# Seven half products for the down projections of combinations 8 to 30, with the rows of two token blocks kept in DRAM

## The reference

```python
x = x + attention(layernorm(x), Wq, bq, Wk, bk, Wv, bv, Wbeta, bbeta, Walpha, balpha)
xt = layernorm(x).reshape(2048, 512)
Wg, Wu, Wd = (LUT[codes] * scales for gate, up, down)      # 4096x512, 4096x512, 512x4096
gate, up = xt @ Wg.T, xt @ Wu.T                            # 2048 x 4096 each
inter = gelu_tanh(gate) * up
x = x + inter @ Wd.T
```

## Time and profile before

| | |
|---|---|
| median of 3 runs | 1143.35 us (1142.88 to 1143.51) |
| span of the profiled execution | 1141.7 us |
| TensorE busy | 1134.5 us, 99% |
| VectorE busy | 709.7 us, 62% |
| GpSimd busy | 553.2 us, 48% |
| ScalarE busy | 450.9 us, 39% |
| chain of work that ended last | 96% TensorE |

### The profile page before, as it was taken

How to read it: one execution, slowest core, us unless ns; L and a number is a source line. 1 busy time by engine, 2 the same in 40 slices (tenths; PEclk the granted TensorE clock), 3 DMA queues, 4 the chain that set the end, 5 groups by cost and what they waited for, 6 DMA issues and landing times.

```text
span 1141.7 us, 20153 instructions
## 1 busy us (share of the span) xinstructions
PE 1134.5 (99%) x8086; PEld 795.0 (70%) x8086; DVE 709.7 (62%) x1306; ACT 450.9 (39%) x1045; POOL 553.2 (48%) x542
## 2 busy tenths in 40 slices
PE   9999999999999999999999999999999999999999
PEld 5666655565467777777777777777777777777786
DVE  7788656367777855665566556655665566555564
ACT  4433334253344434343434343434343434343432
POOL 3386535155783945363636353625362536255430
DMA  8021111000101010101010101010101010000012
GB/s 305 2 76 45 31 38 38 10 10 1 56 19 38 20 38 20 38 19 38 20 37 20 38 19 38 20 37 19 38 21 33 19 36 27 30 18 19 29 38 75
DMA packets 22830, 41.99 MB, mean 37 GB/s; under 512 B 2704, under 2 KB 3024, under 8 KB 22736
## 3 DMA queue, kind: packets, MB, share of 16 engines
q1 hardware_dynamic: 22736, 40.70, 10.9%
HBM read 36.46 MB, written 4.23 MB: 36 GB/s over the span
## 4 chain that ended last, share of the span: by engine, by line
PE 96%; DVE 2%; POOL 1%; issue 0%; DMA 0%; ACT 0%; SPq 0%; DVEq 0%; ACTq 0%; POOLq 0%
PE ps L560 45%; PE ps L665 27%; PE ps L390 8%; PE ps L521 7%; PE ps L625 2%; PE ps L356 1%; PE ps L482 1%; PE ps L465 1%; PE ps L489 1%; PE ps L476 1%; PE ps L400 1%; PE ps L456 1%; DMA WR<-wqkv 0%; POOL bigA L1479 0%; DVE wf L1285 0%
## 5 line engine op out<-in xcount | busy, mean ns | idle before, releaser
L560 PE MATMUL ps<-REG,WR 128*128 128x256 f16 x1344 | 183.3, 273 | 0.0
L560 PE MATMUL ps<-XT,WR 128*128 128x256 f16 x1344 | 183.3, 273 | 0.0
L1302 DVE TENSOR_TENSOR load<-load,ps 128x256 f32<-128x256 f32 x168 | 70.6, 420 | 171.0 <-PE ps L560 100.6
L665 PE MATMUL ps<-WR,ihl_s 128*128 128x512 f16 x720 | 173.0, 379 | 0.0
L665 PE MATMUL ps<-WR,vv 128*128 128x512 f16 x660 | 159.7, 379 | 0.0
L942 ACT COPY load<-ps 128x256 f32<-128x256 f32 x168 | 62.6, 372 | 245.8 <-PE ps L560 245.8
L560 PEld LDWEIGHTS ps<-REG,WR 128*128 128x128 f16 x1344 | 131.4, 98 | 37.5
L560 PEld LDWEIGHTS ps<-XT,WR 128*128 128x128 f16 x1344 | 131.5, 98 | 15.4
L1302 DVE TENSOR_TENSOR bigB<-bigB,ps 128x256 f32<-128x256 f32 x168 | 70.5, 420 | 114.9 <-ACT bigB L942 87.2
L942 ACT COPY bigB<-ps 128x256 f32<-128x256 f32 x168 | 62.6, 373 | 168.8 <-PE ps L560 168.8
L665 PEld LDWEIGHTS ps<-WR,ihl_s 128*128 128x128 f16 x720 | 70.4, 98 | 62.6
(11 more groups left out here) (202 smaller groups left out, 1890.4 us busy)
## 6 DMA issues: line engine op xcount, KB each, us to landing
load<-codes SPq DMA_DIRECT2D x48, 256.0 KB
load<-scales SPq DMA_DIRECT2D x48, 256.0 KB
y<-X SPq DMA_DIRECT2D x15, 256.0 KB, 2.1
bigA<-cla SPq DMA_DIRECT2D x14, 256.0 KB, 3.1
X<-x SPq DMA_DIRECT2D x3, 1024.0 KB, 12.8
WR<-wqkv SPq DMA_DIRECT2D x2, 1024.0 KB, 9.6
X<-x SPq DMA_DIRECT2D x4, 256.0 KB, 4.0
WR<-wqkv SPq DMA_DIRECT2D x4, 256.0 KB, 4.8
```

The costliest lines, as they stand in the source:

```text
L560: mm = eng.matmul(half_bank(kind, name), w(wp, kt), x(xp, kt), start=(first and n == 0), stop=(n == 5), skip_group_check=True)
L665: mm = eng.matmul(PS[bank][:, :], ih[:, ip, 128 * tt:128 * tt + 128], buf[:, wp, at(j), :], start=(j == 0 and p == 0), stop=(j == end and ...
L1302: eng.tensor_tensor(c, c, half_bank(kind, end), ALU.add).then_inc(s_comb, 1)
```

## The change

`SEVEN` becomes combinations 8 to 30: 21 more down projections (8 to 28) are made by seven half products. With it:

- The operands are four parts, e (now both tiles' first halves), o, T01 and T23, in the two tile buffers; each has its own copy and rest.
- The sums of down weights are made for each group from 2 on. So the decode schedule changes: chunks 6g + 6 to 6g + 9 in pairs with m % 8 = 2, 3, 5, 6; the bits of chunk 6g + 10 at 7, its finish at 0; chunk 6g + 5 from its magnitude on at m % 8 = 0, its finish, split, chain and sums at 1. The sums at 4 and 7 stay.
- Room for T and the down sums is taken from X1: it keeps rows of two token blocks. After each combination SP stores its rows in DRAM (`kept`, or the output for 28 and 29), waits, and fills them with those of combination n + 2. VectorE's row updates wait for the fill (`filled`).
- Waits and counts follow (`WHI`, `WLO`, `pair_count`, `finished_in`, `downs_done`).

The core of the diff:

```diff
-SEVEN = (29, 30)
+SEVEN = tuple(range(8, 31))
 SEVEN_PAIRS = tuple(m for n in SEVEN for m in (2 * n, 2 * n + 1))
...
+LAST = 46
+
+
+def plain(k):
+
+    return k < 6 or k in (10, 11, LAST)
+
+
+def second(k):
+    return not plain(k) and k % 2 == 1
+
+
+WHI, WLO = {}, {}
+for _k in range(48):
+    _hi, _lo = (max([0, *(pair[1] for pair in d.values())]) for d in (WHI, WLO))
+    if plain(_k):
+        WHI[_k], WLO[_k] = (_hi + 1, _hi + 2), (_lo + 1, _lo + 2)
+    elif second(_k):
+        WHI[_k] = (_hi + 1, _hi + 2)
+    else:
+        WHI[_k], WLO[_k] = (_hi + 1, _hi + 1), (_lo + 1, _lo + 1)
 
 
 def pair_count(k):
 
-    return 2 * (k // 6 - 1) + k % 6 // 2 + 1
-
-
-def block_kernel(nc, x, wqkv, bqk, bv, wab, bab, codes, scales, out, cla):
+    return k % 6 // 2 + 1 + (3 * (k // 6) - 4 if k >= 12 else 0)
+
+
+def finished_in(k):
+
+    g, c = k // 6, k % 6
+    if k < 12:
+        return k - 2
+    return 8 * g + c - 4 if c > 3 else 8 * g + (-6, -5, -3, -2)[c]
+
+
+def group_of_downs(g):
+
+    return 7 * (4 * g + 4 - SEVEN[0])
+
...
-        tsum = load[:, 0:2, :].bitcast(F32).rearrange("p a (t n) -> p (a t) n", t=2)
+        E2, E3 = (X1[:, t:t + 4, :].rearrange("p t n -> p (t n)") for t in (8, 12))
+        tsum = E2[:, 0:1024].rearrange("p (t n) -> p t n", t=4)
         S1 = [two(WR0[:, a, 7, :]) for a in range(2)]
+
+        def sides(ap):
+            return ap.bitcast(F16).rearrange("p (a k n) -> p a k n", a=2, k=2)
+
+        WDX = [[sides(E3[:, 512 * j:512 * j + 512]) for j in range(3)],
+               [sides(E2[:, 1024:1536]), sides(E2[:, 1536:2048]), sides(tb[:, :])]]
         raw, scl = [load[:, j, :] for j in (0, 2)], [load[:, j, :].bitcast(F32) for j in (1, 3)]
         vals = {"gate": two(load[:, 2:4, :].rearrange("p a n -> p (a n)").bitcast(F32)), "up": two(bigB[:, 1024:2048])}
...
-                    pe.wait_ge(s_wsum, pair_count(SUMMED))
-                part = {"P1": "e", "P2": "o", "P3": "o"}.get(name, "T")
-                at = {"P3": 1, "P6": 1, "P7": 2, "P4": 3}.get(name, 0)
+                    pe.wait_ge(s_wsum, pair_count(k))
+                part, at = {"P1": ("e", 0), "P2": ("e", 1), "P5": ("T01", 0), "P6": ("T01", 1), "P3": ("o", 0),
+                            "P7": ("T23", 0), "P4": ("T23", 1)}[name]
                 pe.wait_ge(s_olo, operand(2 * n + us[-1], part))
 
                 def weight(wp, u):
-                    if name in ("P5", "P6", "P7", "P3"):
-                        side = {"P6": 0, "P7": 1, "P3": 2}
-                        return S1[wp][:, u, :] if name == "P5" else wide("down", 7, wp, side[name])[:, u, :]
-                    row = WR1[:, wp, (8 if name == "P1" else 10) + u, :].rearrange("p (v e n) -> p v e n", v=2, e=2)
-                    return row[:, :, 1 if name == "P4" else 0, :]
+                    if name in ("P6", "P7", "P3"):
+                        return wide("down", g, wp, {"P6": 0, "P7": 1, "P3": 2}[name])[:, u, :]
+                    if name == "P5" and k == LAST + 1:
+                        return S1[wp][:, u, :]
+                    row_ = buf[:, wp, (8 if name in ("P1", "P5") else 10) + u, :]
+                    return row_.rearrange("p (v e n) -> p v e n", v=2, e=2)[:, :, 1 if name in ("P4", "P5") else 0, :]
 
                 for tt in tts:
                     for u in us:
...
+                n, u = m // 2, m % 2
                 ac.wait_ge(s_inter, whole(2 * m))
-                ac.wait_ge(s_prod, pair_base("up", 55, 7) + 7)
-                if m // 2 > SEVEN[0]:
-                    ac.wait_ge(s_dn, 4 * SEVEN[0])
-                eng.copy(part_of(m, 0, "e")[:, 0, :], fw[:, 0, 0:256]).then_inc(s_ohi, 1)
-                eng.copy(part_of(m, 0, "o"), two(fw[:, 1, :])).then_inc(s_ohi, 1)
+                if n > SEVEN[0]:
+                    ac.wait_ge(s_seven, seventh(n - 1, "P4" if u else "P6"))
+                else:
+                    ac.wait_ge(s_dn, row_done(n - 1 if u else n - 2, 3))
+                eng.copy(part_of(m, 0, "e"), part_from("e")).then_inc(s_ohi, 1)
+                eng.copy(part_of(m, 0, "o"), part_from("o")).then_inc(s_ohi, 1)
 
             def sums_high(m):
-                ac.wait_ge(s_dsum, 4 * (m - SEVEN_PAIRS[0]) + 4)
-                eng.copy(part_of(m, 0, "T"), tsum).then_inc(s_ohi, 1)
+                for part in ("T01", "T23"):
+                    ac.wait_ge(s_dsum, 4 * (m - SEVEN_PAIRS[0]) + 4)
+                    eng.copy(part_of(m, 0, part), part_from(part)).then_inc(s_ohi, 1)
 
             def act_tile(i):
...
-                paired = m % 8 in (4, 7)
+                paired = m % 8 in (4, 7) and m < 56
+                if m % 8 == 1 and m > 9:
+                    paired, k = True, 6 * (m // 8) + 5
                 snapshot("gate", m, "P1")
...
                 ac.wait_ge(s_prod, pair_base("gate", m, 7) + PRODUCT["P4"])
                 gelu(oo, half_bank("gate", "P4"))
-                if paired and m < 56:
+                if m % 8 == 1 and m > 9:
+                    dequant(k)
+                if paired:
                     dq_sums(k, 0, 2)
-                if m == 59:
-                    dq_sums(SUMMED, 0, 2)
                 snapshot("up", m, "P1")
                 ac.wait_ge(s_comb, done + COMBINED["C12"])
...
+                if m % 8 == 0 and m > 8:
+                    dequant(6 * (m // 8) + 4)
                 snapshot("up", m, "P7")
-                if not paired and dk < 48:
-                    dequant(dk)
-                    dk += 1
+                for c in range(10, 48):
+                    if finished_in(c) == m and (c < 12 or c % 6 < 4):
+                        dequant(c)
             inter_high(NI - 1)
...
                 inter_low(i)
 
+            def filled(n):
+                if n >= 6:
+                    dv.wait_ge(s_fill[n % 2], 16 * ((n - 6) // 2 + 1))
+
             def gather(n, tt):
-                T = 4 * (n % 4) + tt
+                T = row(n, tt)
                 dv.wait_ge(s_dn, row_done(n, tt))
+                filled(n)
                 eng.scalar_tensor_tensor(X1[:, T, :], PS[bank_of["dn", n, tt]][:, :], 1.0 / (WS * IS), X1[:, T, :],
                                          ALU.mult, ALU.add).then_inc(s_ev, 1)
 
...
                 e, o, at = fw[:, 0, :], fw[:, 1, :], 4 * (m - SEVEN_PAIRS[0])
                 if m > SEVEN_PAIRS[0]:
-                    dv.wait_ge(s_olo, operand(m - 1, "T"))
+                    dv.wait_ge(s_olo, operand(m - 1, "T23"))
+                else:
+                    dv.wait_ge(s_kept[0], 16)
                 dv.wait_ge(s_inter, whole(2 * m))
...
                 oo, ee, n = 2 * m + 1, 2 * m, m // 2 - 1
                 if m > 8:
                     rows_of_second(m - 1)
-                done = pair_base("up", m, 3)
+                done, g = pair_base("up", m, 3), m // 8
+                downs = m > 9 and m % 8 < 2
+                bits, rest = (), ()
+                if m < 10:
+                    bits = rest = (m + 2,)
+                elif m < 56 and m % 8 in (2, 3, 5, 6):
+                    bits = rest = (6 * g + 6 + (0, 0, 0, 1, 0, 2, 3)[m % 8],)
+                elif m < 56 and m % 8 == 7:
+                    bits = (6 * g + 10,)
                 combine("gate", m, "C11")
-                bits = (m == 8 or m % 8 not in (0, 5)) and dk < 48
-                if bits:
-                    dq_magnitude(dk)
+                if downs and m % 8 == 1:
+                    dq_finish(6 * g + 5)
+                for k in bits:
+                    dq_magnitude(k)
                 combine("gate", m, "C22")
                 if m in (9, 11):
...
                     gather(n, 2 * m % 4)
-                if bits:
-                    dq_sign(dk)
+                for k in bits:
+                    dq_sign(k)
+                if downs and m % 8 == 0:
+                    dq_finish(6 * g + 4)
                 combine("up", m, "C11")
-                if m % 8 not in (4, 7) and dk < 48:
-                    dq_finish(dk)
-                    dk += 1
+                for k in rest:
+                    dq_finish(k)
...
                 if n in SEVEN and m % 2 == 0:
                     into_rows(n, "P5")
+                if downs and m % 8 == 0:
+                    dq_magnitude(6 * g + 5)
                 combine("up", m, "C22")
                 dv.wait_ge(s_comb, done + COMBINED["C22"])
...
                     into_rows(n, ("P6", "P4")[m % 2])
+                if downs and m % 8 == 0:
+                    dq_sign(6 * g + 5)
                 combine("up", m, "C12")
                 dv.wait_ge(s_comb, done + COMBINED["C12"])
                 inter(ee, vals["up"][:, 0, :], piece(m, "even"))
...
                     operands_low(m - 1)
                 elif m > 8:
                     inter_low(2 * m - 1)
                     inter_low(2 * m - 2)
-                if m == 58:
-                    dq_difference(SUMMED)
-                    dq_chain(SUMMED)
-                if m == 59:
-                    dq_sums(SUMMED)
```

(92 more changed lines are left out.)

118 lines of the change are left out of this document (50 added, 68 removed).

## The result

The changed kernel takes 1205.62 us (median of 4, 1202.39 to 1208.37), the kernel before 1143.3: a ratio of 1.0544, interval 1.0531 to 1.0557, slower. The forecast was 1196 us, in a range of 1165 to 1223.

What follows compares the result with a forecast made beforehand. The matmul engine bounds the kernel, busy 1134.5 of 1141.7 us; -25 + 26 + 15 + 31 + 6 = +53 us gave a span of 1194.7, and with 1.65 for the median 1196 us, range 1165 to 1223.

Steps and rivals of the forecast that it cites:

- The gain: Combinations 8 to 28: 21 new seven-product ones, each 1.19 us less matmul time, 25.0 us saved.
- Pairs m % 8 = 4 and 7: Ten pairs with a chain: up P6 waits 2.6 us behind ScalarE's copy and GpSimd's chain, 26 us.
- Pairs m % 8 = 0: Six pairs: VectorE's magnitude waits for the code load, so up P3 waits for C22; 15 us.
- Pairs m % 8 = 1: Six pairs: late VectorE and GpSimd work holds up P6 by 5.0 us, P7 by 0.1; 31 us.
- late handover: Pairs m % 8 = 1: VectorE's operand sums end at 5.9 instead of 4.6; gate P3 waits 1.0 us.
- Pairs with a decode: Twenty pairs, m % 8 = 2, 3, 5, 6: operand sums delay C22 before gate P3, 0.3 us each, 6 us.
- Hidden edits: Row stores and fills in DRAM, waits on kept rows, moved buffers and new counts: cost 0.
- The sum: All terms together: -25 + 26 + 15 + 31 + 6 = +53 us.
- rival D: TensorE's clock falls in new idle times in pairs m % 8 = 1: +21, 1217 us; chance 0.06.
- Rival A: Only the chain is on the path, loads land early and VectorE catches up: +24, 1167 us; chance 0.15.
- Rival B: Waits hidden because GpSimd ends the operands at 5.5 instead of 8.05: faster, 1120 us; chance 0.07.
- Rival C: VectorE becomes the bound, each of the twenty decode pairs costs 1.2 us more: 1220 us; chance 0.10.

Runs made afterwards that it cites:

- experiment 7: As experiment 5, but VectorE makes the magnitude after combine C22 of gate in every pair with a decode; 1117.2 us, ratio 0.977 to the kernel before.
- Experiment 1: Changed kernel with ScalarE's four copies of the weight sums moved behind the snapshot of up P7; 1192.94 us.
- experiment 2: Changed kernel with a separate buffer for the raw codes of chunk 6g + 5, loaded two pairs ahead; 1191.96 us.
- experiment 4: Changed kernel without the stores of rows to DRAM, the fills and their waits (those of 28 and 29 to the output stay); 1205.78 us.
- experiment 3: Changed kernel with useless matmuls put before TensorE's long waits from pair 20 on; 1197.07 us.
- experiment 5: Changed kernel, same work reordered on ScalarE, GpSimd and VectorE, with waits per rest and a separate raw buffer for chunk 6g + 5; 1132.14 us, ratio 0.9902.

## Why the prediction was right, point by point

- **The gain** of 25.0 us: right. It is in the changed kernel too (pair 28 holds 14.41 of work), and experiment 7 shows it alone.
- **Pairs m % 8 = 4 and 7**: 26 us forecast, 2.40 and 2.21 each measured, 23 us, by the chain as written down: up P6 was put at about 11.7 after the start and starts at 11.73 and 11.64. Experiment 1 shows the cause: the waits go when the copies leave their place.
- **Pairs m % 8 = 0**: 15 us forecast, 15.9 measured. The cause is shown by experiment 2. The load took 4.4 and not 3.8 us, and magnitude 1.4, the low end of what I gave it.
- **Pairs m % 8 = 1**: 31 us forecast, too much. The waits are 2.9 to 3.1 us at up P6 and 0.8 at gate P3 in three of the six, 21 us in all. Short delays add to that: pair 41 of experiment 4, which has no slow stretch, takes 17.39 against 13.10 us of work, so the six cost about 26 without the clock, by my estimate. The rows of pair 41 of the changed kernel (start 839.23) show where the forecast went wrong, VectorE's last operand sum, GpSimd's first chain step, and the two waits of TensorE:

```profile
844.21 0.78 DVE L1309 TENSOR_TENSOR X<-fw,X 128x256 f32<-128x256 f32 x1
```

```profile
850.38 1.26 POOL L1632 TENSOR_TENSOR wf<-wf,bigC 128x512 f32<-128x512 f32 x1
```

```profile
846.90 0.39 PE L611 MATMUL ps<-XT,bigB 128*128 128x256 f16 x2 [0.81 <-DVE load L1363]
852.62 0.83 PE L611 MATMUL ps<-REG,bigA 128*128 128x256 f16 x6 [2.92 <-ACT bigB L1003]
```

  The late handover is real: the sums end at 5.8, where I had 5.9 (pair 25 comes out of a slow pair and has them at 5.2). Gate P3 waits 0.8 and not 1.0. What I had wrong comes after it. My own terms, 8.9 + 2.5 + 1.35, make 12.75 and not the 13.2 that I wrote for the end of the chain step, and it ends at 12.4; the late snapshot of gate P6 holds gate P7 up by 0.1 and not 0.5. Up P6 starts at 13.4, and I had 14.15. The figure without the handover has a slip too: 12.8 - 9.17 is 3.6 and not 3.8.
- **Pairs with a decode**: 6 us forecast, about 0.1 us each measured, and a wait of 0.93 in pair 26. GpSimd was idle beside magnitude in nearly all of them, and its first step took 0.68, not 1.02. The cost that I had in mind exists, but here other waits covered it: once they are gone, gate P3 waits for C22 for 0.9 us in pairs m % 8 = 2 (experiments 3 and 5) and for 0.4 and 0.6 in pairs 3 and 5 (experiment 5), and moving the magnitude saves 15 us (experiment 7).
- **Hidden edits**: nothing that can be measured, as experiment 4 shows.
- **The sum** of the waits was 78 us and came out at 61 of long waits and some 10 of small ones. What brought the time above the forecast is rival D, at a chance of 0.06: the clock. Its price of 21 us is close to the 19 of the balance, but experiment 3 gives back 11 between the profiled executions and 8.5 between the medians. It was not confined to the 3.5 us waits either, as I had it: the clock fell after waits of 2.2 to 2.4 us as well. The two misses, waits too high by about 7 and the clock left out, partly cancelled: it is luck that the total came out nearer than the terms.
- **Rival A** (only the chain) was wrong about the load. **Rival B** did not happen: GpSimd ends the operands at 8.2, as summed. Its 1120 us are reached in experiment 7, but by another way: there GpSimd still ends them at 8.2 (pair 28), and the snapshot no longer stands behind a copy that waits for the chain. **Rival C** fell: at 78% busy VectorE keeps up once its steps stand where it is idle.

## What to carry to other kernels

When side work is added to a kernel whose matmul engine is full, averages of the other engines say little: follow one round instruction by instruction and ask of each copy that frees a bank what stands before it in its queue, and what that waits for. A loss of 62 us turned into a gain of 26 with the same work and one more buffer for codes, by moving copies that nobody waits for behind those that the matmuls wait for, by waiting for parts and not for the whole, and by placing decode steps in idle time. After such an edit look again, since the backlog shows up at the next reader.
